# Attention and experts on one core: two heads side by side on 64 contraction rows each, scores issued in pairs

## What is computed

```python
qkv = x @ in_proj_w.T + in_proj_b
q, k, v = jnp.split(qkv, 3, axis=-1)          # to_heads: [b, 16, 1024, 16]
scores = jnp.einsum('bhqd,bhkd->bhqk', q * scale, k) + mask   # 0 in the allowed band, -1e9 or so outside
out = jnp.einsum('bhqk,bhkd->bhqd', jax.nn.softmax(scores, axis=-1), v)
x = _layernorm(x + out @ out_proj_w.T + out_proj_b)
x = _layernorm(x + moe(x))
```

## Time and profile before

| | us |
|---|---|
| median of 3 runs (1290.63 to 1294.56) | 1293.54 |
| profiled execution, first to last instruction | 1287.9 |
| projection, to about | 100 |
| attention, about 100 to 680 | 580 |
| experts, from about 680 | 608 |

### The profile page before, as it was taken

One profiled execution on the slowest core, in us unless ns is written; L12 is line 12 of the kernel. 1 busy time (PEld: TensorE's weight loads), 2 busy tenths in 40 slices (PEclk: granted clock), 3 DMA queues, 4 the chain that ended last, 5 costly groups with the idle time before them and its releaser, 6 DMA issues.

```text
span 1287.9 us, 28066 instructions
## 1 busy us (share of the span) xinstructions
PE 1214.8 (94%) x8448; PEld 644.6 (50%) x8448; DVE 947.5 (74%) x1975; ACT 625.9 (49%) x1366; POOL 238.9 (19%) x432
## 2 busy tenths in 40 slices
PE   7877999999999999999799999898998989989997
PEld 4543444444444444443356666565665656556564
DVE  7587888888888888887657776676776767757754
ACT  4415777777777777777633332323222232222332
POOL 8831222222222222222401010010200102000000
PEclk9998999999999999999999999898999999999999
DMA  5631111111111111110131232121312212122220
GB/s 166 187 116 53 38 39 39 37 37 37 37 37 37 37 34 32 34 36 14 46 84 61 48 99 59 61 71 43 90 49 63 77 51 90 50 47 77 59 82 33
DMA packets 62443, 76.78 MB, mean 60 GB/s; under 512 B 8992, under 2 KB 37408, under 8 KB 62368
## 3 DMA queue, kind: packets, MB, share of 16 engines
q1 hardware_dynamic: 60736, 72.80, 19.2%
q10 hardware_dynamic: 1632, 3.15, 0.8%
HBM read 62.94 MB, written 12.85 MB: 59 GB/s over the span
## 4 chain that ended last, share of the span: by engine, by line
PE 64%; DVE 13%; issue 9%; ACT 7%; SPq 2%; POOL 2%; DMA 2%; DVEq 0%; ACTq 0%; POOLq 0%
PE bank L759 16%; PE bank L604 11%; PE bank L572 9%; PE bank L587 9%; PE bank L772 9%; DVE hf L1192 3%; DVE sg L1185 3%; ACT hh L947 3%; ACT a_PT L863 3%; PE bank L647 2%; PE bank L575 2%; PE bank L688 1%; PE bank L628 1%; PE bank L651 1%; SPq L324 1%
## 5 line engine op out<-in xcount | busy, mean ns | idle before, releaser
L984 DVE TENSOR_REDUCE a_mx<-bank 128x1 f32<-128x512 f32 (+3 forms) x720 | 401.2, 618 | 73.7 <-PE bank L575 44.6
L863 ACT ACTIVATE a_PT<-bank 128x512 f32<-128x512 f32 (+4 forms) x832 | 357.0, 505 | 138.1 <-PE bank L587 137.5
L587 PE MATMUL bank<-a_QS,a_KS 113*128 113x512 f16 (+4 forms) x832 | 269.6, 331 | 11.4 <-ACT a_PT L863 6.1
L572 PE MATMUL bank<-a_KS,a_QS 112*128 112x512 f16 (+4 forms) x832 | 258.6, 332 | 15.5 <-DVE a_mx L984 8.3
L947 ACT CAST hh<-hf 128x512 f16<-128x512 f32 x144 | 89.0, 618 | 332.5 <-DVE hf L1192 332.5
L509 POOL TENSOR_SCALAR_AFFINE_SELECT a_PT<-a_PT 128x256 f32<-128x256 f32 (+1 forms) x288 | 109.6, 381 | 419.0 <-ACT a_PT L863 418.7
L604 PE MATMUL bank<-a_PT,a_VG 128*17 128x512 f32 (+4 forms) x1664 | 179.7, 504 | 6.4 <-POOL a_PT L509 6.4
L772 PE MATMUL bank<-dh,hh 128*128 128x256 f16 x576 | 159.0, 276 | 16.9 <-DVE z L1207 16.9
L1199 DVE TENSOR_TENSOR hl<-hf,hh 128x512 f16<-128x512 f32 x144 | 99.8, 693 | 99.4 <-ACT hh L947 99.4
L772 PE MATMUL bank<-dh,hl 128*128 128x256 f16 x576 | 159.1, 276 | 0.0
L772 PE MATMUL bank<-dl,hh 128*128 128x256 f16 x576 | 159.1, 276 | 0.0
(11 more groups left out here) (134 smaller groups left out, 1438.2 us busy)
## 6 DMA issues: line engine op xcount, KB each, us to landing
cb<-c_dram SPq DMA_DIRECT2D x128, 256.0 KB, 3.3
q_dram<-p_qk SPq DMA_DIRECT2D x32, 128.0 KB, 2.1
k_dram<-p_qk SPq DMA_DIRECT2D x32, 128.0 KB, 2.1
a_QS<-q_dram SPq DMA_DIRECT2D x64, 64.0 KB
a_KS<-k_dram SPq DMA_DIRECT2D x64, 64.0 KB
xb<-x SPq DMA_DIRECT2D x8, 512.0 KB, 3.6
out<-oo SPq DMA_DIRECT2D x8, 512.0 KB, 4.2
p_xf<-xT ACTq DMA_DIRECT2D x6, 512.0 KB, 4.2
```

Of the source, the lines that this page charges most:

```text
L572: mm = pe.matmul(bank[:, at:at + hi - lo], QS[p][0:MR, t // NT, h, t % NT * P:t % NT * P + P], KS[p][0:MR, piece, h % 2, 0:hi - lo], start ...
L587: pe.matmul(stbank[u % 3][:, 0:(qc + 1) * CH - q0], KS[p][0:MR + 1, kt // NT, h % 2, kt % NT * P:kt % NT * P + P], QS[p][0:MR + 1, qc, h, ...
L863: act.activation(PT[(p + i) % 2][:, h, 0:w], stbank[u % 3][:, 0:w], ACT.Exp)\
L984: dve.tensor_reduce(mx[:, piece, t // NT, heads[0]:heads[0] + n, t % NT], sbank[u % 3][:, 0:n * w].rearrange("p (h k) -> p h k", h=n), AX. ...
```

## The change

Heads on rows 0 to 63 and on rows 64 to 127 are now separate matmuls of 48 rows (`KR`; 49 for transposed scores) that start at partition 0 or 64 (`lane`). `QS` halves in width, and nothing needs zeros any more. The mask operands must lie on each lane: `idb` and `tri` have two parts of 64 rows each, so that a mask of 128 columns is two matmuls (128 and 64 columns). The rows of lane 64 of `tri` are built in a new tile `late` and copied by DVE. Heads alternate between lanes (`heads_of`, `max_units`), the unit (3, 1) of all four heads is split in two (46 units), and TensorE issues per slot T T S S T T, W, then the rest of the S.

```diff
-MR = 112
+KR = 3 * HD
...
-                n = {1: 1, 2: 2, 3: 2}.get(CH // (hi - lo), HG)
-                units += [(t, piece, lo, hi, range(h, h + n)) for h in range(0, HG, n)]
+                firsts = (2, 0) if CH // (hi - lo) > 1 else (2, 0, 3, 1)
+                n = HG // len(firsts)
+                units += [(t, piece, lo, hi, range(h, h + n)) for h in firsts]
...
+def heads_of(slot):
+    units = share(slot)
+    first = UNITS[units[0][0]][4][0] if units else HG // 2
+    return (0, 2, 1, 3) if first >= HG // 2 else (2, 0, 3, 1)
+def lane(h):
+    return 64 * (h // 2)
...
             def put_max(G, p, half):
                 sp.wait_ge(s["mT_done"], G * NH2 + half + 1)
-                sp.dma_start(QS[p][MR:MR + 1, half, :, :].rearrange("o h t -> o (h t)"), mT[half][:])\
-                  .then_inc(negmax[half][p], 16)
+                for e in range(2):
+                    at, n = 64 * e + KR, HG // 2 * NT
+                    sp.dma_start(QS[p][at:at + 1, half, :, :].rearrange("o i t -> o (i t)"),
+                                 mT[half][n * e:n * e + n]).then_inc(negmax[half][p], 16)
...
-            for a in (KS[0], KS[1]):
-                pool.memset(a[:], 0.0).then_inc(s["stack_zero"], 1)
...
-                wait(pe, s["max_done"], G * NU + u - 2)
+                wait(pe, s["max_done"], G * NU + (u - 2 if u >= 3 else LAST_MAX[u] - NU + 1))
...
-                    mm = pe.matmul(bank[:, at:at + hi - lo], QS[p][0:MR, t // NT, h, t % NT * P:t % NT * P + P],
-                                   KS[p][0:MR, piece, h % 2, 0:hi - lo], start=True, stop=(m1 <= m0))
+                    mm = pe.matmul(bank[:, at:at + hi - lo], QS[p][r:r + KR, t // NT, h % 2, t % NT * P:t % NT * P + P],
+                                   KS[p][r:r + KR, piece, h % 2, 0:hi - lo], start=True, stop=(m1 <= m0))
+                    for part in range(2):
+                        f0 = max(c0, 64 * part)
+                        if c1 > f0:
+                            mm = pe.matmul(bank[:, at + f0 - c0 + m0 - lo:at + hi - lo], idb[r:r + 64, part, :],
+                                           tri[r:r + 64, part, f0:c1], start=False, stop=(part == 1 or c1 <= 64))
...
-            pe.wait_ge(s["tri_done"], 2)
+            pe.wait_ge(s["tri_done"], 9)
...
-                    for h in range(HG):
-                        scoresT(G, p, k, i, h)
-                        some_scores(rest[h:h + 1] if h < HG - 1 else ())
+                    for n in range(0, HG, 2):
+                        scoresT(G, p, k, i, n)
+                        scoresT(G, p, k, i, n + 1)
+                        some_scores(rest[n:n + 2] if n == 0 else ())
                     if i:
                         weighted(G, p, i - 1)
-                    some_scores(rest[HG - 1:])
+                    some_scores(rest[2:])
...
-            for a in (QS[0], QS[1]):
-                dve.memset(a[:], 0.0).then_inc(s["stack_zero"], 1)
...
-            dve.wait_ge(s["stack_zero"], 4)
             for a in KS:
-                dve.memset(a[96:P], 1.0).then_inc(s["stack_const"], 2)
+                for r in (32, 96):
+                    dve.memset(a[r:r + 32], 1.0).then_inc(s["stack_const"], 1)
+            dve.wait_ge(s["tri_done"], 8)
+            dve.tensor_copy(tri[64:P], late[64:P]).then_inc(s["tri_done"], 1)
```

More of the change, by code:

```diff
@@ L66, in share @@
     return [((n - TAIL) % NU, n >= TAIL) for n in range(lo, hi)]
+def heads_of(slot):
+    units = share(slot)
+    first = UNITS[units[0][0]][4][0] if units else HG // 2
+    return (0, 2, 1, 3) if first >= HG // 2 else (2, 0, 3, 1)
+HEADS = [heads_of(i) for i in range(NSL)]
+def lane(h):
+    return 64 * (h // 2)
 def settle(eng, sem):
@@ L182, in attention_memory @@
     v_all = sb("v_all", [P, NR, S // P, VW], F32)
-    QS = [sb(f"QS{p}", [P, NH2, HG, CH], F16) for p in range(2)]
+    QS = [sb(f"QS{p}", [P, NH2, HG // 2, CH], F16) for p in range(2)]
     KS = [sb(f"KS{p}", [P, NH2, HG // 2, CH], F16) for p in range(2)]
     VG = [sb(f"VG{p}", [P, S // P, VW], F32) for p in range(2)]
-    idb = sb("idb", [P, P], F16)
-    tri = sb("tri", [P, P], F16)
+    idb = sb("idb", [P, 2, P], F16)
+    tri = sb("tri", [P, 2, P], F16)
+    late = sb("late", [P, 2, P], F16)
     mx = sb("mx", [P, 2, NH2, HG, NT], F32)
@@ L193, in attention_memory @@
     PT = [sb(f"PT{p}", [P, HG, CH], F32) for p in range(2)]
-    return v_all, QS, KS, VG, idb, tri, mx, mT, OTs, rec, raw, PT
+    return v_all, QS, KS, VG, idb, tri, late, mx, mT, OTs, rec, raw, PT
 def expert_memory(sb):
@@ L254, in program @@
     NST = NSL * HG
+    LAST_MAX = [max(u for u in range(NU) if u % 3 == n) for n in range(3)]
     LAST_OF = [max(u for u in range(NST) if u % 3 == n) for n in range(3)]
@@ L907, in body @@
                 for i in range(NSL):
-                    for h in range(HG):
-                        exp(G, p, i, h)
+                    for n in range(HG):
+                        exp(G, p, i, n)
                     if i == 0 and not (isinstance(G, int) and G == 0):
```

70 lines of the change are left out of this document (40 added, 30 removed).

## The result

The changed kernel takes 1428.99 us (1423.86 to 1443.24, four runs) where the kernel before takes 1292.29 in the same comparison: a ratio of 1.108, with an interval of 1.102 to 1.114. It is slower, as forecast, but by 136.7 us instead of 26.5, and 91 us above the upper end of the range.

The account below looks back on a forecast made before the run. The prediction took the 1.18 us loop through an exponential, not TensorE's columns, to limit wide slots. Start 10.0 us plus groups' scores 16.5 us made 26.5, added to 1293.5: 1320 us, range 1294 to 1338.

Parts of the forecast that it names:

- anything beyond (the drains, a lower granted clock): Whole run: chance of 0.05 kept for causes outside the forecast and its rivals, such as mode-change drains or a lower clock.
- The start, 10.0 us: Before the projection: TensorE waits for DVE's fills and mask copy, starting 10.6 us later, less 0.6 us given back.
- rival 4: Start: its delay is swallowed because the projection later waits for transfers, giving 1310 us; chance 0.06.
- The loop of 1.18 us: Wide attention slots: the fourth T waits for an exponential, so first to fourth T takes at least 1.18 us.
- The wide slot's 2.84 us: Attention before the change: the time a wide slot costs TensorE, about 2.84 us, against DVE 2.2 and ACT 1.9.
- Rival 1: Attention scores: overlapping lanes save their columns, 5.2 us a group, giving 1225 us; chance 0.09.
- The S behind W, net 1.10 us a group: Attention groups: more S behind W lose 2.09 us, a shorter first to fourth T gains 0.99; 16.5 us over 15.
- the forecast of 34.2: Attention: a group, from one `maxT` to the next, would take about 34.2 us.
- my whole sum of 26.5: Whole run: 10.0 us for the start plus 16.5 us for the groups' scores.
- Masked pairs: Scores with masks: the pair overlaps only in the last piece, 0.42 us for 320 columns, 0.52 for 448.
- Slot 1's bank: Group start: with 46 units the first S shares the last unit's bank and waits; first to fourth T 1.67 to 1.94.
- The changes of mode: Around `maxT` and `outT`: 0 to 8 gaps of 0.10 us a group, 0 to 12 us in all, taken as 0.

Follow-up runs that it names:

- e4_pairs_only: Kernel before, with its 112 and 113 rows, given only the changed kernel's order T T S S T T W: 1317.09 us, ratio 1.0204.
- e6_one_lane: Changed kernel with every head's scores on lane 0, so no two matmuls run at once: 1736.3 us, ratio 1.3461.
- e10_64_rows: Changed kernel with each score matmul over all 64 rows of its lane, and four fills of `QS` at the start: 1388.18 us, ratio 1.0766.
- e17_all_48: `e14_all` with scores over 48 and 49 rows in place of 64, its fills left in: 1334.14 us, ratio 1.0263.
- e14_all: Changed kernel with early mask copy, 48 units, 64-row scores, old order T S T S T S T W S, and DVE's merge ahead of slot 1's maxima: 1308.78 us.
- e3_double_t: Changed kernel with every transposed score (T) issued twice, 832 matmuls more: 1403.07 us, ratio 1.0875.
- e11_filler: Changed kernel with one extra matmul of 128 rows and 256 columns ahead of each pair of T: 1406.19 us, ratio 1.0877.
- e16_half_double: `e14_all` with every second T issued twice, 416 matmuls more: 1302.16 us, ratio 1.0075.
- e5_singles: Changed kernel in the order of the kernel before, T S T S T S T W S: 1379.62 us, ratio 1.0677.
- e9_narrow_s: Kernel before with only S cut to 48 rows of one lane, T left at 113 rows: 1422.34 us, ratio 1.1024.
- e1_start: Changed kernel with the fills of `KS[0]` and the copy of `tri` moved ahead of `winl`: 1425.95 us, ratio 1.1047.
- e2_banks: Changed kernel with 48 units a group instead of 46, so a group's first S doesn't share a bank with the last: 1390.8 us, ratio 1.0789.
- e13_singles_64: Changed kernel with early mask copy, 48 units, 64-row scores and the old order T S T S T S T W S: 1326.98 us, ratio 1.0284.

## Why the prediction was wrong

**The step that failed** is a sentence of the part "How the numbers follow": "anything beyond (the drains, a lower granted clock) 0.05". The sum took every duration from rows at full clock, and so supposed that the clock would stay as it was. In the attention it fell to half for nearly half of the time. So a group took 40.8 us and not 34.2, and DVE's share fell to 67% (153.28 of 230 us) and not to 80%. From the rows of after: a mean of 0.77 in 530 us means 0.46 of them, 244 us, at half; 0.69 in 60 us means 37; 0.86 in 120 us means 34. Together 315 us. The slots above, 4.33 us at half and 2.8 at full, put the lost share of that time at 0.35: 111 us, an estimate. They are two different slots, so here are two whole groups of after as well, a slow and a fast one:

```profile
324.10:369.12 45.02, 42.13 (x282) 13.99 (x281) 27.63 (x62) 23.91 (x59) 7.22 (x19) 0.66 0.09 26
702.62:742.00 39.38, 35.89 (x290) 12.66 (x282) 28.16 (x62) 24.12 (x59) 7.21 (x19) 0.83 0.07 21
```

The first has 30.6 us at half and the second 13.4: 17.2 more, for which it takes 5.64 longer, a share of 0.33. Beside it stand 136.7 - 26.5 = 110 us, the measured loss less what the order costs at full clock (`e4_pairs_only`). W's mean says the same: (802 - 607) / (1026 - 607) = 0.47 of its matmuls at half clock, if 1026 ns, its mean in `e6_one_lane`, stands for the half level.

What brings the fall about is shown in part. More rows without more columns raise the clock (`e10_64_rows`; `e17_all_48` against `e14_all`), and so do more matmuls (`e3_double_t`, `e11_filler`, `e16_half_double`) and an order that spreads them (`e5_singles`). Being busy doesn't hold it or bring it back (`e6_one_lane`), the order alone doesn't lower it (`e4_pairs_only`). So in these runs the clock rose with the rows in use and with the matmuls issued, and the change leaves each score matmul 48 or 49 of its 112 or 113 rows while a slot at full clock still takes as long. `e9_narrow_s` kept its clock with narrow S. How the chip decides stays open.

**The start, 10.0 us.** The place was right to the tenth, though in part by terms that cancel (the last fill ends at 18.57 and not 18.73, the copy takes 0.22 and not 0.3, and TensorE starts 0.26 after it): the fills and the copy of DVE, then TensorE:

```profile
16.81 1.76 DVE L1007 MEMSET a_KS<- 32x2048 f16 x1 [0.48 <-issue]
18.61 0.22 DVE L1009 COPY a_tri<-a_late 64x256 f16<-64x256 f16 x1
```

```profile
19.09 1.01 PE L680 MATMUL bank<-p_xh,p_winh 128*128 128x512 f16 x2 [19.09 <-DVE a_tri L1009]
```

At the first `maxT` after is 11.3 us later than before (97.1 against 85.8), as the term had it. How much of it reaches the end is open: the edit that returns the first matmul to 8.06 gives 7 us at the first `maxT`, and 3 us, not told from zero, at the end (`e1_start`), at a clock that is lower by 0.02. So rival 4, that something swallows the delay, is neither shown nor ruled out.

**The loop of 1.18 us** from first to fourth T was right: 399.73 - 398.58 = 1.15 us in after at full clock, with the fourth T waiting for an exponential. (The wide slot's 2.84 us lies 0.03 under its own terms, 1.32 + 0.32 + 1.00 + 0.23; nothing hangs on it.) Rival 1 so fell, although its mechanism is real: the lanes do run at once, 0.22 us a pair, and it brings nothing here, as the loop had it.

**The S behind W, net 1.10 us a group.** `e4_pairs_only` has the same order and measures 1.8 us a group, 26.5 us in all. That kernel's lanes don't overlap, so more S lie bare. For the changed kernel at full clock no run gives the number; an estimate from the two groups above is 39.38 - 0.33 x 13.4 = 35.0 us, 1.9 over before, and the forecast of 34.2 isn't far from it. The likeness of 26.5 to my whole sum of 26.5 is a coincidence: mine had 10 of them in the start.

**Masked pairs** were wrong, in the kernel's favour. I had them one behind the other, 0.42 us for 320 columns. In after the S pair starts at 401.05 and the next T at 401.28: 0.23 us with four mask matmuls. The two S start 10 ns apart, so the second head's S doesn't wait behind the first one's mask, and "matmuls start in the order of the program" doesn't hold across the lanes. It isn't always so: the pair at 441.64 has its second S at 441.83 and the next T at 442.03, 0.39 us. "I am wrong if masked pairs start together": some do.

**Slot 1's bank** was seen, and under-priced: the prediction let the slot grow by 0.27 us (1.67 to 1.94); the wait at 415.12 is 0.72, and the attention without it is 12 us shorter, 0.8 a group (`e2_banks`). **The merge of the maxima** was missed. I named the maximum that comes later, but not that `maxT` waits for a merge that stands on DVE behind it. The waits of TensorE in after (engine, line, releaser: us, times, longest):

```profile
PE bank L601 <- DVE a_mx L1018: 27.2, 47, 4.2
PE bank L619 <- ACT a_PT L897: 21.6, 54, 1.4
PE bank L806 <- DVE z L1241: 19.5, 5, 4.0
PE bank L680 <- DVE a_tri L1009: 19.1, 1, 19.1
PE bank L649 <- DVE a_mx L1026: 16.2, 15, 1.1
```

The last row is 16.2 us in 15 groups; before has no such row. In `e13_singles_64` it is 8.4 us, and `e14_all`, without it, is 18 us faster. **The changes of mode**, kept at 0 to 12 us, have 0.10 us each by `e9_narrow_s`, the size that the gap ahead of W gave; at one `maxT` of after two of them can be read: S at 403.75, `maxT` at 404.07, T at 404.28, so 0.32 us ahead of it and 0.21 behind, where before has 0.12 behind (378.81 to 378.93). Their sum over all `maxT` and `outT` wasn't measured.

**What the stages add up to.** The attention of after is 130 us longer than before. The half clock there, 0.44 of 686.6 us against 0.02 of 556.8, is 291 us more, at 0.35 an estimate of 102 us; the order adds the 27 of `e4_pairs_only`. In `e14_all` the same reckoning puts 34 of its 47 us to the clock, and in `e16_half_double`, with 416 matmuls more, 9 of 42: the other 13 and 33 us stay open.

## What to carry to other kernels

Before a matmul is cut to fewer rows so that two can share the array, ask whether the stage is bound by TensorE's columns. If it isn't, nothing is gained, and the granted clock may be lost with everything that runs between, W and the transposes too. Read the clock by stretch for the changed kernel first of all, and try zero rows up to the full lane before giving up. Compare stage by stage and not by the total: an edit here changed by 28 us a stage that it doesn't touch. When an order of issue changes, follow each consumer of a maximum to the instruction behind which its merge stands.
